# Attention joined over its batches, early first loads, and the turned maxima split by GpSimd

## The chip, the cores and the metric

The kernel runs on one core of a Trainium2 chip. The metric is the device time of one execution in microseconds. Three runs of the kernel before gave 2043.46, 2043.80 and 2047.93 us, a median of 2043.8 us.

## What is computed

The input `x` is 4 batches of 1024 tokens with 128 channels. Four residual layers follow one another: an attention with 16 heads of 8 channels, a mixture of experts, a gated delta layer with convolutions, and the same mixture of experts again. The change touches the first layer alone:

```python
x = x + attn_a(layernorm(x))
    q, k, v = x @ Wq.T, x @ Wk.T, x @ Wv.T          # 16 heads of 8
    q_c, k_c = q - mean(q), k - mean(k)             # over the 8 channels
    cov = einsum('bhqd,bhkd->bhqk', q_c, k_c) / 8
    var = outer(sum(q_c^2) / 7, sum(k_c^2) / 7) / 8
    attn = softmax(cov + var, axis=-1)
    out = (attn @ v) @ Wo.T
x = x + moe(layernorm(x)); x = x + attn_b(layernorm(x)); x = x + moe(layernorm(x))
```

A head's score is thus a product over 9 rows (8 channels and the variance). The rows are kept in three bf16 parts each, and 81 products of parts stand one below the other, so that one bf16 matmul gives the score with nearly the accuracy of f32.

## The kernel before, in words

**The projection, `project_qkv`.** 8 chunks of 512 tokens. Each chunk is normalised, turned and projected; ScalarE and VectorE split q, k and the variances into three bf16 parts, and SyncE's queue stores the parts in DRAM (`scr.terms`), four transfers for each chunk: two at L424, two at L428. The part tiles are double, so ScalarE waits before chunk c until the transfers of chunk c - 2 have landed (`s_out`). GpSimd meanwhile clears rows 64 to 127 of the operand tiles `q_op` and `k_op` (L311) and sets three rows of `k_op` to one (L315). The block ends when all transfers have landed.

**The attention, `attend`.** A unit is one batch with four heads (`GH`); there are 16 units, u = 4 b + s. The loads of a unit (L524 and L528) are 12 transfers, three of 216 KB and nine of 72 KB. In a unit:

- `scores_for_max` (L567): 32 tiles of 128 queries by 1024 keys, 8 matmuls each, into two buffers of `ps_max`; `reduce_max` (L696) takes the negated maximum of each query on VectorE. TensorE writes a tile when the reduction of the tile two before is done (`s_maxed`). This runs 40 tiles ahead (one unit and `LEAD` = 8).
- `turn_max` (L621) transposes the 32 columns of maxima. `split_max` (L707 to L714, VectorE) copies them out of PSUM and splits them into three bf16 parts by five operations that each need the one before. `max_rows` (L535) has SyncE's queue put the three parts as three rows into `q_op`, so that the second scores come out with the maximum subtracted.
- `scores_for_prob` (L582): 64 tiles of 128 keys by 512 queries, 4 matmuls each, into two buffers of `ps_prob`. The first of a unit waits for the three rows (`s_nmrow`). ScalarE takes the exponential (L684) into a ring of 16 tiles.
- `pv` (L599): the exponentials times v, four heads in four strips of `ps_acc`. A unit has two halves of 512 queries; each half sums over 8 key tiles.
- After a half, ScalarE copies `ps_acc` to SBUF in two pieces (`copy_acc`, L667), TensorE turns it by four matmuls with 36 columns of the identity (`combine`, L611) into `ps_misc`, and VectorE divides by the row sums (`normalise`, L719 and L725).

**The order.** TensorE's stream is written out by hand in 32 steps for each unit. Step i holds the two halves of one max tile, two probability tiles, one after the other in turn, and one piece of `pv` that lies `PV_LAG` = 3 steps back. As there is a single `ps_acc`, the first piece of a half (due in steps 3 and 19) is held back and made together with the second in steps 4 and 20, behind the wait for `copy_acc`. `combine` follows in the same steps, `turn_max` of the next unit in step 25. ScalarE puts the copies before exponentials 7 and 8 of a half, VectorE puts `normalise` in steps 6 and 22 and `split_max` in step 26.

**The loop over batches.** `batches` writes out batch 0 and batch 3 and puts batches 1 and 2 into a loop of the hardware (`Fori`), on every engine, with offsets and semaphore values in registers. So units 0 to 3 and 12 to 15 are straight code, and units 4 to 11 are two passes of one body.

## Time and profile before

| | |
|---|---|
| median of three runs | 2043.8 us |
| the profiled execution, its own time | 2043.38 us |
| its span on the core | 2041.7 us |
| projection, last transfers landed | about 92 us |
| attention, first loads to last operation | 92 to 912 us |
| TensorE matmul, busy over the span | 1361.8 us (67%) |
| VectorE | 1540.1 us (75%) |
| ScalarE | 917.1 us (45%) |
| GpSimd | 227.3 us (11%) |

The table of the page has the busy time of an engine over the whole span. It is an average over layers that are bound by different engines, so it only says where to look: in the 820 us of the attention, TensorE, VectorE and ScalarE all show nine tenths or seven to nine tenths of each slice. Which of them sets the pace has to be read from the idle time of the others and from what ended it. A row of the timeline has the start in us, the time in us to the end of the last of its instructions, the engine (PE is TensorE, PEld its weight load, DVE VectorE, ACT ScalarE, POOL GpSimd, SP SyncE; a q behind it marks its sequencer), the line, the tiles and shapes, the count, and in brackets the idle time before it with what released it.

### The profile page before, as it was taken

The page shows a single profiled execution, that of the slowest core. Times are in us where ns is not written, and L with a number is a line of the kernel's source. Part 1 is how long each engine was busy: PE and PEld are TensorE (multiplying, and loading weights), DVE is VectorE, ACT ScalarE, POOL GpSimd, SP SyncE. Part 2 cuts the span into 40 slices and gives each one's busy share as a digit, 9 for nine tenths or more (in the row PEclk, how much of TensorE's full clock was granted, in tenths as well). Part 3 has the DMA queues.
Part 4 walks back from the last instruction along what each step waited for, and adds up shares of the span by engine and source line. Part 5 has one row for each costly group of instructions (what it writes and reads, how often), then busy time and mean ns, then how long its engine had stood idle before and what let it go on. Part 6 is the DMA issues. An engine that isn't in the chain of part 4 may idle for free. (4 is left out here: it accounts for less than half of the span.)

```text
span 2041.7 us, 44670 instructions
## 1 busy us (share of the span) xinstructions
PE 1361.8 (67%) x15216; PEld 723.2 (35%) x15216; DVE 1540.1 (75%) x3117; ACT 917.1 (45%) x2009; POOL 227.3 (11%) x218
## 2 busy tenths in 40 slices
PE   4489999999999999984399674000000078841998
PEld 2214444444444444443166442000000024420665
DVE  5598888888788888707166576899999899972665
ACT  4507777777677777774143273001222200030343
POOL 6000000000000000003414300000000000025044
PEclk9858999999999999997699876555555589965999
DMA  3430111111111110003224415810222010012243
GB/s 98 120 80 5 40 41 30 29 29 29 30 29 29 29 29 3 3 20 96 60 55 66 75 67 117 212 41 10 63 63 54 19 41 0 0 43 58 55 67 44
DMA packets 118670, 101.05 MB, mean 49 GB/s; under 512 B 23665, under 2 KB 100018, under 8 KB 118066
## 3 DMA queue, kind: packets, MB, share of 16 engines
q1 hardware_dynamic: 101570, 84.79, 16.2%
q0 software_dynamic: 11264, 8.92, 3.0%
q10 hardware_dynamic: 5616, 4.47, 1.3%
q8 instruction: 130, 2.13, 0.4%
q14 instruction: 90, 0.74, 0.1%
HBM read 55.98 MB, written 31.21 MB: 43 GB/s over the span
## 5 line engine op out<-in xcount | busy, mean ns | idle before, releaser
L696 DVE TENSOR_REDUCE att_negmax<-att_ps_max 128x1 f32<-128x1024 f32 x512 | 613.9, 1221 | 112.5 <-PE att_ps_max L567 91.8
L684 ACT ACTIVATE att_probs<-att_ps_prob 128x512 f32<-128x512 f32 x1024 | 561.4, 598 | 244.7 <-PE att_ps_prob L582 233.8
L567 PE MATMUL att_ps_max<-av_k_op,av_q_op 81*32 81x512 bf16 x4096 | 418.0, 404 | 43.1 <-DMA av_q_op<-terms_q 18.9
L582 PE MATMUL att_ps_prob<-av_q_op,av_k_op 99*32 99x512 bf16 x4096 | 406.9, 385 | 9.2 <-ACT att_probs L684 1.2
L599 PE MATMUL att_ps_acc<-att_probs,att_vq 128*32 128x256 f32 x4096 | 308.3, 381 | 0.0
L1926 PE MATMUL out_ps_y<-all_bo_row,all_ones 1*128 1x128 f32 x2 | 0.8, 482 | 372.8 <-PEq L104 372.8
L567 PEld LDWEIGHTS att_ps_max<-av_k_op,av_q_op 81*32 81x32 bf16 x4096 | 109.4, 98 | 184.2 <-DVE att_negmax L696 80.6
L582 PEld LDWEIGHTS att_ps_prob<-av_q_op,av_k_op 99*32 99x32 bf16 x4096 | 108.1, 95 | 174.1 <-ACT att_probs L684 129.7
L599 PEld LDWEIGHTS att_ps_acc<-att_probs,att_vq 128*32 128x32 f32 x4096 | 126.4, 111 | 82.3 <-issue 5.8
L1145 ACT ACTIVATE moe_moe_gate<-moe_moe_ps_h 128x256 f32<-128x256 f32 x122 | 46.8, 383 | 214.2 <-PE moe_moe_ps_h L1086 214.2
L1926 PEld LDWEIGHTS out_ps_y<-all_bo_row,all_ones 1*128 1x128 f32 x2 | 0.5, 305 | 373.1 <-issue 373.1
L1086 PE MATMUL moe_moe_ps_h<-all_w_all,moe_moe_xgT 128*128 x244 | 128.0, 607 | 1.4 <-DVE moe_moe_xgT L1286 1.4
L1310 DVE TENSOR_TENSOR moe_moe_y<-moe_moe_y,moe_moe_ps_y 128x128 f32 x182 | 52.4, 288 | 89.3 <-issue 81.0
L1835 ACT ACTIVATE solve_p<-solve_state,solve_decay 128x32 f32<-128x32 f32 x128 | 45.0, 351 | 155.7 <-DVE solve_state L1819 155.7
L1101 PE MATMUL moe_moe_ps_y<-all_w_all,moe_moe_hT 128*128 x728 | 111.6, 276 | 0.3
L1101 PEld LDWEIGHTS moe_moe_ps_y<-all_w_all,moe_moe_hT 128*128 128x128 f32 x728 | 95.7, 192 | 1.5 <-issue 1.5
L1286 DVE COPY moe_moe_xgT<-moe_moe_ps_g 128x256 f32<-128x256 f32 x92 | 38.2, 415 | 69.4 <-PE moe_moe_ps_g L1079 69.4
L511 POOL COPY att_vq<-av_v 128x288 f32<-128x288 f32 (+1 forms) x16 | 6.8, 427 | 728.6 <-PE att_ps_acc L599 728.5
L1079 PE MATMUL moe_moe_ps_g<-all_ident,moe_moe_xin 128*128 128x128 f32 x182 | 36.5, 280 | 69.8 <-DMA moe_moe_xin<-expert_rows 69.6
L1944 PE MATMUL out_ps_o<-out_qS,out_gather 128*128 128x512 f32 x128 | 65.0, 632 | 25.8 <-DVE out_qS L2035 25.7
L1302 DVE SCALAR_TENSOR_TENSOR moe_moe_hs<-moe_moe_gate,moe_moe_scale,moe_moe_ps_h 128x256 f32<-128x256 f32 x122 | 58.3, 478 | 20.2 <-ACT moe_moe_gate L1145 20.0
L2029 DVE TENSOR_TENSOR_SCAN out_St<-b_a,out_kd 128x1024 f32<-128x1024 f32 x32 | 73.1, 2284 | 0.4
(277 smaller groups left out, 2067.4 us busy)
## 6 DMA issues: line engine op xcount, KB each, us to landing
moe_moe_xin<-expert_rows SPq DMA_DIRECT2D x182, 72.0 KB, 1.8
av_k_op<-terms_k SPq DMA_DIRECT2D x48, 216.0 KB
av_q_op<-terms_q SPq DMA_DIRECT2D x144, 72.0 KB
solve_dec_and_windows<-solve_Xw SPq DMA_DIRECT2D x16, 256.0 KB, 3.0
solve_dec_and_windows<-solve_k SPq DMA_DIRECT2D x16, 256.0 KB, 3.7
terms_q<-qkv_parts_q SPq DMA_DIRECT2D x8, 384.0 KB, 2.6
terms_k<-qkv_parts_k SPq DMA_DIRECT2D x8, 384.0 KB, 3.2
all_w_all<-in_f_w SPq DMA_DIRECT2D x24, 128.0 KB, 2.5
```

The source lines that it names most:

```text
L567: mm = pe.matmul(ps_max[c * STRIP:(c + 1) * STRIP, a % 2, k * CH:(k + 1) * CH], q_op[s][0:R_ALL, h, at:at + STRIP], k_op[s][0:R_ALL, h, k ...
L582: mm = pe.matmul(ps_prob[c * STRIP:(c + 1) * STRIP, j % 2, :], k_op[s][0:R_END, h, at:at + STRIP], q_op[s][0:R_END, h, half * CH:(half + 1 ...
L599: mm = pe.matmul(ps_acc[32 * h:32 * h + 32, cols], vq[:, s % 2, kt, VW * h:VW * h + 32], probs[:, (GH * v + h) % PROBS, cols], start=(kt = ...
L684: act.activation(probs[:, j % PROBS, :], ps_prob[:, j % 2, :], ACT.Exp).then_inc(s_exp, 1)
L696: dve.tensor_reduce(negmax[:, s % 2, a:a + 1], ps_max[:, a % 2, :], AX.X, ALU.max, negate=True).then_inc(s_maxed, 1)
L1086: pe.matmul(ps_up[n % 3][:, :, :].rearrange("p w f -> p (w f)"), xgT[:, n // 2 % 3, cols], wall[:, bass.ds(at0, 2 * F)], start=True, stop= ...
L1101: mm = pe.matmul(ps_y[n % 2][:, 0:P], hT[:, n % 3, i * P:(i + 1) * P], wall[:, bass.ds(at0 + (2 * F + i * P), P)], start=(i == 0), stop=(i ...
L1145: act.activation(gate[:, n % 3, :], ps_up[n % 3][:, 0, :], ACT.Silu).then_inc(s_silu, 1)
L1302: dve.scalar_tensor_tensor(out=hs[:, n % 3, :], in0=gate[:, n % 3, :], scalar=scale[:, n:n + 1], in1=ps_up[n % 3][:, 1, :], op0=ALU.mult, ...
L1310: dve.tensor_tensor(tile, tile, ps_y[n % 2][:, 0:P], ALU.add).then_inc(s_sum, 1)
L1944: mm = pe.matmul(ps_o[:, i * CH:(i + 1) * CH], gather[:, e, :, :].rearrange("p h d -> p (h d)"), qS[:, e % 2, i * CH:(i + 1) * CH], start= ...
L2029: dve.tensor_tensor_scan(St[:, e % 2, :], a[:, tok], kd[:, e % 2, :], 0.0, ALU.mult, ALU.add).then_inc(s_S, 1)
```

## The change

- `batches` is a Python loop over all four batches: no loop of the hardware is left in `attend`, on any engine. The store loop of `project_qkv` is written out too.
- The loads of units 0 and 1 are issued on SyncE's queue within `project_qkv`: eight transfers (two groups of `load_terms`) after each of the stores of chunks 2, 3 and 4. Before the first of them the queue waits for the stores of chunks 0 and 1 and for all of GpSimd's clearing. `attend` loads units 2 and 3 at its start.
- `ps_acc` becomes two banks, one for each half; `ps_misc` is gone. The first piece of `pv` is made in its own step. `combine` is four transposes of 128 columns that write into the bank of the half itself; `turn_max` writes into the bank of the first half.
- The pieces of `copy_acc` stand before exponentials 6 and 8.
- The turned maxima are copied by ScalarE (`take_max`), before exponential 54 of a unit (step 27), and the five operations of the split run on GpSimd (`split_max`), behind its copy of v.
- `normalise` is one reciprocal and one product where it was one reciprocal and four products.

The diff, cut to its core:

```diff
+            early = [(s, i) for s in range(EARLY) for i in range(NPART)]
+            for c in range(NC_):
+                store(c)
+                if c == 2:
+                    for p in range(2):
+                        sp.wait_ge(s_out[p], 16 * NDMA)
+                    sp.wait_ge(s_ones, 1 + 3 * NQ)
+                if c >= 2:
+                    for s, i in early[2 * (c - 2):2 * (c - 1)]:
+                        load_terms(sp, g, scr, 0, s, i)
...
+EARLY = 2
...
-COPY_AT = 2 * PV_LAG + 1
+COPY_AT = 2 * PV_LAG
...
-        ps_acc = m.ps("ps_acc", [P, CH])
-        ps_misc = m.ps("ps_misc", [P, CH])
-        comb = ps_misc[:, P:P + CT * GH * VW].rearrange("p (t g r) -> p t g r", t=CT, g=GH)
+        ps_acc = [m.ps(f"ps_acc{half}", [P, CH]) for half in range(2)]
+        comb = [a[:, :].rearrange("p (t g r) -> p t g r", t=CT, g=GH) for a in ps_acc]
...
-            body(0, True, False)
-            with eng.Fori(1, last_b) as b:
-                body(b, False, False)
-            body(last_b, False, True)
+            for b in range(B):
+                body(b, b == 0, b == last_b)
...
+            def split_max(u):
+
+                pool.wait_ge(s_split, u + 1)
+                if u >= 2:
+                    pool.wait_ge(s_nmrow, 16 * NPART * (u - 1))
+                chain = Count(pool, s_nmch, 4 * u)
+                rows, rest, parts = nm_rows[:, :], nm_rest[:, :], nm_parts[:, u % 2]
+                chain.done(pool.tensor_copy(parts[:, 0, :], rows))
+                chain.done(pool.tensor_tensor(rest, rows, parts[:, 0, :], ALU.subtract))
+                chain.done(pool.tensor_copy(parts[:, 1, :], rest))
+                chain.done(pool.tensor_tensor(rows, rest, parts[:, 1, :], ALU.subtract))
+                pool.tensor_copy(parts[:, 2, :], rows).then_inc(s_nmp, 1)
...
-                    if kt == 0 and not (isinstance(b, int) and b == 0 and s == 0 and half == 0):
-                        pe.wait_ge(s_acc, 2 * u + half)
+                    if kt == 0:
+                        if half == 0:
+                            pe.wait_ge(s_split, u + 1)
+                        elif u:
+                            pe.wait_ge(s_norm, 2 * u)
...
-                    mm = pe.matmul(comb[:, t], acc_sb[:, half, t * P:(t + 1) * P],
-                                   g.ident[:, :].rearrange("p (g r) -> p g r", g=GH)[:, :, 0:VW],
-                                   start=True, stop=True)
+                    mm = pe.transpose(ps_acc[half][:, t * P:(t + 1) * P], acc_sb[:, half, t * P:(t + 1) * P],
+                                      g.ident[:, :])
...
-                        for w in (w - 1, w) if w % (2 * TB) == 1 else () if w % (2 * TB) == 0 else (w,):
-                            if w >= 0:
-                                pv(b, s, w // 2, w % 2)
-                            elif not (first and s == 0):
-                                pv(*prev(b, s), (w + STEPS) // 2, w % 2)
+                        if w >= 0:
+                            pv(b, s, w // 2, w % 2)
+                        elif not (first and s == 0):
+                            pv(*prev(b, s), (w + STEPS) // 2, w % 2)
...
+            def take_max(u):
+                act.wait_ge(s_nmT, u + 1)
+                if u:
+                    act.wait_ge(s_nmp, u)
+                act.activation(nm_rows[:, :], ps_acc[0][0:STEPS, 0:P], ACT.Copy).then_inc(s_split, 1)
...
-                        if COPY_AT <= j <= COPY_AT + 1 and not (first and s == 0):
-                            copy_acc(*prev(b, s), 1, j - COPY_AT)
+                        if j == 2 * (STEPS - LEAD + 3) and not (last and s == NQ - 1):
+                            take_max(u + 1)
+
+                        if j in (COPY_AT, COPY_AT + 2) and not (first and s == 0):
+                            copy_acc(*prev(b, s), 1, (j - COPY_AT) // 2)
...
-                        if i == STEPS - LEAD + 2 and not (last and s == NQ - 1):
-                            split_max(*nxt(b, s, 1))
```

## Rows read from the trace of the kernel before

**Rows 1.** Waits from 150 to 1060 us: who waited for whom, total us, times, longest.

```profile
ACT att_probs L684 <- PE att_ps_prob L582: 233.8, 386, 60.9
```

**Rows 2.** Timeline of ScalarE in two steps of unit 2.

```profile
282.76 1.08 ACT L684 ACTIVATE att_probs<-att_ps_prob 128x512 f32<-128x512 f32 x2 [0.22 <-PE att_ps_prob L582]
...
284.07 1.09 ACT L684 ACTIVATE att_probs<-att_ps_prob 128x512 f32<-128x512 f32 x2 [0.22 <-PE att_ps_prob L582]
```

**Rows 3.** A stretch of unit 2: length, busy us of PE, PEld, DVE, ACT, POOL.

```profile
294.10:296.00 1.90, 1.90 (x40) 1.00 (x36) 1.89 (x2) 1.46 (x4) 0.00 (x0) 1.00 0.00 0
```

**Rows 4.** L684 alone, from unit start to unit start (units 2, 7, 8, 9).

```profile
250.25:297.16 46.91, 35.04 (x65) 1.00 0.14 32
...
486.34:538.16 51.82, 35.04 (x65) 0.99 0.16 39
538.16:588.75 50.59, 35.36 (x65) 0.95 0.08 19
588.75:636.01 47.26, 35.04 (x64) 1.00 0.12 31
```

**Rows 5.** Timeline of steps 3 and 4 of unit 2, the change of halves.

```profile
254.17 0.60 ACT L684 ACTIVATE att_probs<-att_ps_prob 128x512 f32<-128x512 f32 x1 [0.22 <-PE att_ps_prob L582]
...
255.40 0.41 ACT L667 ACTIVATE att_acc_sb<-att_ps_acc 128x256 f32<-128x256 f32 x1
...
255.66 1.12 ACT L684 ACTIVATE att_probs<-att_ps_prob 128x512 f32<-128x512 f32 x2
...
256.95 1.08 PE L611 MATMUL att_ps_misc<-all_ident,att_acc_sb 128*128 128x36 f32 x8
...
257.96 0.40 PE L567 MATMUL att_ps_max<-av_k_op,av_q_op 81*32 81x512 bf16 x4
...
258.63 1.08 ACT L684 ACTIVATE att_probs<-att_ps_prob 128x512 f32<-128x512 f32 x2 [1.84 <-PE att_ps_prob L582]
```

**Rows 6.** Timeline of four transposes in the projection and what follows.

```profile
75.95 0.66 PE L355 MATMUL qkv_ps_x<-all_ident,qkv_xn 128*128 128x128 f32 x4 [1.07 <-ACT qkv_xn L324]
76.54 0.63 PE L377 MATMUL qkv_ps_var<-qkv_square_q,all_varsel 128*48 128x512 f32 x1
```

**Rows 7.** Timeline around the split of the maxima in unit 2.

```profile
289.74 0.27 DVE L707 COPY att_nm_rows<-att_ps_misc 32x128 f32<-32x128 f32 x1
...
291.31 7.29 DVE L696 TENSOR_REDUCE att_negmax<-att_ps_max 128x1 f32<-128x1024 f32 x6
291.41 1.78 SPq L535 DMA_DIRECT2D av_q_op<-att_nm_parts  x3
...
293.24 1.09 ACT L684 ACTIVATE att_probs<-att_ps_prob 128x512 f32<-128x512 f32 x2 [1.16 <-PE att_ps_prob L582]
```

**Rows 8.** GpSimd's groups up to 400 us: busy us, mean ns, idle before.

```profile
L179 POOL TENSOR_SCALAR_AFFINE_SELECT all_varsel<-all_varsel 128x16 f32<-128x16 f32 x16 | 3.2, 198 | 2.2
L511 POOL COPY att_vq<-av_v 128x288 f32<-128x288 f32 x4 | 1.7, 426 | 159.4 <-PE att_ps_acc L599 159.3
```

**Rows 9.** Line L535, the three rows of maxima: durations in ns, and time to landing.

```profile
L535 SPq DMA_DIRECT2D av_q_op<-att_nm_parts x48: 502/584/1269, 145.1 to 864.7; - x48
...
DMA to landing us min/median/max: 1.8/1.8/3.0
```

**Rows 10.** Timeline at the end of the first pass of the loop.

```profile
536.98 0.62 PE L567 MATMUL att_ps_max<-av_k_op,av_q_op 81*32 81x512 bf16 x4 [3.64 <-issue]
```

**Rows 11.** Timeline of the start of the attention, and GpSimd's clearing before it.

```profile
37.15 14.20 POOL L315 MEMSET av_k_op<- 3x4096 bf16 x4
...
92.25 0.29 SPq L524 DMA_DIRECT2D av_k_op<-terms_k  x1
...
103.80 1.90 PE L567 MATMUL att_ps_max<-av_k_op,av_q_op 81*32 81x512 bf16 x16 [18.86 <-DMA av_q_op<-terms_q]
```

**Rows 12.** Stretches: us, engines' busy us, then PEclk, DMA share, GB/s.

```profile
73.00:78.00 5.00, 3.93 (x19) 1.97 (x17) 2.22 (x5) 4.27 (x10) 0.00 (x0) 1.00 0.58 177
...
100.00:104.00 4.00, 0.20 (x4) 0.14 (x8) 0.00 (x0) 0.00 (x0) 0.00 (x0) 0.50 0.61 162
```

More of the change, by code:

```diff
@@ L430, in _, with store @@
-            repeat(sp, NC_ // 2, body)
+            def store(c):
+                i, p = c // 2, c % 2
+                tok = slice(c * CH, (c + 1) * CH)
+                for w in range(2):
+                    sp.wait_ge(s_p3[w][p], i + 1)
+                    sp.dma_start(scr.terms[w][:, 0:D, :, tok].rearrange("i d h t -> (d h) i t"),
+                                 parts[w][:, p, :, :]).then_inc(s_out[p], 16)
+                sp.wait_ge(s_v3[p], i + 1)
+                for w in range(2):
+                    sp.dma_start(scr.terms[w][:, D, :, tok].rearrange("i h t -> h i t"),
+                                 vparts[32 * w:32 * w + H, p, :, :]).then_inc(s_out[p], 16)
@@ L435, with load_terms @@
+def load_terms(sp, g, scr, b, s, i):
+    heads, tok, row = slice(s * GH, (s + 1) * GH), slice(b * S, (b + 1) * S), i * NPART * K1
+    sp.dma_start(g.k_op[s][row:row + NPART * K1, :, :],
+                 scr.terms[1][:, :, heads, tok].rearrange("j d h t -> (j d) h t")).then_inc(g.s_load[s], 16)
+    for j in range(NPART):
+        sp.dma_start(g.q_op[s][row + j * K1:row + (j + 1) * K1, :, :],
+                     scr.terms[0][i, :, heads, tok]).then_inc(g.s_load[s], 16)
 LEAD = 8
 PV_LAG = 3
-COPY_AT = 2 * PV_LAG + 1
+COPY_AT = 2 * PV_LAG
@@ L536, in max_rows @@
                                  nm_parts[:, s % 2, i, :]).then_inc(s_nmrow, 16)
-            for s in range(NQ):
+            for s in range(EARLY, NQ):
                 load(0, s)
@@ L577, in scores_for_prob @@
                     pe.wait_ge(s_nmrow, 16 * NPART * (u + 1))
-                if not (isinstance(b, int) and b == 0 and s == 0 and j < 2):
+                if not (b == 0 and s == 0 and j < 2):
                     pe.wait_ge(s_exp, 2 * STEPS * u + j - 1)
@@ L618, in turn_max @@
                 pe.wait_ge(s_maxed, STEPS * (u + 1))
-                if not (isinstance(b, int) and b == 0 and s == 0):
-                    pe.wait_ge(s_misc, 3 * u - 1)
-                pe.transpose(ps_misc[0:STEPS, 0:P], negmax[:, s % 2, :], g.ident[:, :]).then_inc(s_nmT, 1)
+                if not (b == 0 and s == 0):
+                    pe.wait_ge(s_norm, 2 * u - 1)
+                pe.transpose(ps_acc[0][0:STEPS, 0:P], negmax[:, s % 2, :], g.ident[:, :]).then_inc(s_nmT, 1)
             for a in range(STEPS):
@@ L652, in body @@
                             turn_max(*nxt(b, s, 1))
-            batches(pe, body)
+            batches(body)
             for w in range(STEPS - PV_LAG, STEPS):
                 pv(last_b, NQ - 1, w // 2, w % 2)
-            combine(last_b, NQ - 1, 1, last=True)
+            combine(last_b, NQ - 1, 1)
         @block.scalar
@@ L693, in reduce_max @@
                 dve.wait_ge(s_scored, STEPS * u + a + 1)
-                if a == 0 and not (isinstance(b, int) and b == 0 and s < 2):
+                if a == 0 and not (b == 0 and s < 2):
                     dve.wait_ge(s_nmT, u - 1)
@@ L2097, in build @@
         g.s_experts = m.sem("experts_loaded")
+        g.s_load = m.sems("terms_loaded", NQ)
         g.s_scat = m.sem("rows_scattered")
```

101 lines of the change are left out of this document (32 added, 69 removed).

## The prediction

> **What bounds the kernel now.** The chain that ended last covers only the final layer, so it says nothing here; I read the attention in three steps. First the waits: ScalarE stood idle 233.8 us in all before its exponentials, each time for TensorE's scores [rows 1]. Then the inside of a step: exponentials start at 282.76 and 284.07, 1.31 us apart, with 0.22 us of idle time before each pair [rows 2], and over 1.90 us TensorE is busy 1.90, VectorE 1.89 and ScalarE 1.46 [rows 3]. TensorE sets the pace and VectorE is just behind it: with only two buffers of max tiles, any extra work of VectorE beyond about half a us comes back as a stall of TensorE. Third, the units: a unit of straight code takes 46.91 us, one of the loop 47.26, and the two on either side of the jump back take 51.82 and 50.59 [rows 4]. Were a unit only its 32 steps, it would take 32 x 1.305 = 41.8 us. So 5.1 us of each unit lie between steps, and the change goes at these.
>
> **Change of halves (twice in a unit).** The exponentials of steps 3 and 4 start 258.63 - 254.17 = 4.46 us before the next step where two steps are 2.61: 1.85 us extra [rows 5]. Of it 1.01 us (256.95 to 257.96) is the eight matmuls of `combine` [rows 5]; the other 0.84 is TensorE running into ScalarE, since step 3 has no `pv` and the double piece in step 4 waits for both copies out of the one `ps_acc`. After the change `pv` has another bank and waits for nothing that is late: the maxima were read in step 27 of the unit before, and for the second half `normalise` ran in step 6. The copies cost ScalarE 0.26 us each (255.40 to 255.66 [rows 5]) against 0.22 us of idle time in a step [rows 2], so about 0.04 us is left over, which the double buffer takes. `combine` becomes four transposes; the same four in the projection, at the same clock, took 76.54 - 75.95 = 0.59 us to the next matmul [rows 6]. The second copy is done before exponential 8, a whole step's TensorE work ahead of `combine`. So a change of halves costs 0.62 us in place of 1.85: 1.23 less. There are 31 within the units (unit 0 has one): 31 x 1.23 = 38.1 us. In the last three, where no max tiles are left and ScalarE sets the pace, the gain is a little larger; I add 0.7. Sum 38.8. Bounds: as little as nothing of the 0.84 may go if another wait takes its place (then only 0.42 is gained each, 13 us), and no more than the whole 1.85 less 0.59 (39 us).
>
> **The split of the maxima leaves VectorE.** Six operations hold VectorE from 289.74 to 291.31, 1.57 us, and the exponentials two steps later have 1.16 us of idle time before them in place of 0.22: 0.94 us lost [rows 7, 2]. This stall goes in units 0 to 13 (in unit 14 VectorE has no tiles at that point): 14 x 0.94 = 13.2 us. ScalarE takes one copy of 32 x 128. It reads half the columns of the copy that cost 0.26 us [rows 5], so it fits in 0.22 us of idle time: taken at nothing, at most 0.05 x 15. Its wait is for a transpose that TensorE issued at the end of step 25, two steps earlier; only exponentials are queued behind it.
>
> **The new chain.** GpSimd now stands between the copy and the three rows. What is late next is SyncE's queue and then the first probability tile of the next unit, and all of TensorE's stream queues behind that one wait. The time there is: the copy before exponential 54 ends near 289.75, so GpSimd starts at about 289.85. The next unit starts at 297.16 [rows 4], its first probability tile 0.44 us earlier, and without the 0.94 stall that is 295.8. The three transfers take 2 x 0.6 us of issuing and then 1.8 us to land, 3.0 us [rows 7, 9]. That leaves 295.8 - 3.0 - 0.1 - 289.85 = 2.85 us for five dependent operations. The trace has no such operation on GpSimd. Its copy of 128 x 288 takes 0.43 us, a select of 16 columns 0.20, and dependent selects have 2.2 / 16 = 0.14 us between them [rows 8]. Between these two rows a copy of 128 columns is about 0.30 us. An operation with two inputs is unknown: from 0.28 us (as the row of 0.30 with nothing added) to 0.85 (twice the largest row). In all, 3 x 0.30 + 2 x (0.28 to 0.85) + 4 x 0.14 = 2.0 to 3.2 us. I take 0.45 each, near the one-input rows, since 128 columns are few beside the fixed part: 2.4 us, so no stall and 0.4 us to spare. GpSimd has nothing else in that stretch; its copy of v for the next unit was done early in the unit. A rule speaks against this edit: the Trainium skill, GPSIMD Engine Reference, section Performance versus the Vector engine, finds an operation with two inputs 1.96 times as long on GpSimd as on VectorE. No row of this trace shows one. By it each of the two would be an estimated 0.55 us and the sum unchanged, with a reserve of some 0.2 us.
>
> **The loop goes.** The two units at the jump back took 51.82 + 50.59 - 2 x 47.26 = 7.9 us more than their like; at the jump TensorE stood 3.64 us for nothing that the profile shows [rows 4, 10], and the granted clock of the next unit was 0.95. Straight units do not have this. The eight loop units are 0.35 us longer than straight ones [rows 4]: 2.8 us. Together 10.7. Longer code could stall in its fetching, but the eight straight units of before, which differ from the new ones only in number, have no such gap, so I add nothing.
>
> **Normalise and turn_max.** One product in place of four shortens a burst on VectorE that was nearly hidden. Beyond halves and split, 46.91 - 41.8 - 3.70 - 0.94 = 0.5 us is left in a straight unit, some 0.3 of it the transpose, which stays; I take 0.1 a unit, 1.5 us. In 43.4 us a unit, VectorE has 32 reductions at 1.21 us (7.29 us for six [rows 7]) and about 1.2 us more, 40 in all, so it stays behind TensorE.
>
> **The early loads.** The attention starts at 92.25 and TensorE's first scores at 103.80, released by the loads [rows 11]. With units 0 and 1 loaded the first scores start at about 92.4: 11.4 us less. The clock there is 0.50 [rows 12], and I leave it so, since TensorE still stands idle from the end of the projection. The price is on the queue in the projection. A chunk lasts 8 us; its stores are 0.88 MB at up to 177 GB/s, 5 us; two groups of loads are 0.88 MB at 162 GB/s, 5.5 us [rows 12]. So three chunks bring 10.5 us of transfers in 8, and the queue falls behind by some 2.5 us each, 7.5 at the most, and makes it good in the chunks 5 to 7. ScalarE waits for stores two chunks old, which have about 8 us of reserve, so I take nothing. If the loads share the engines worse than this, chunk 7 waits up to 3 us. The wait for the clearing costs nothing: it ends at 37.15 + 14.20 = 51.35 [rows 11], when the queue has just issued chunk 2's stores. `attend` now issues two unit loads fewer, and its own two are needed tens of us later.
>
> **The sum.** 38.8 + 13.2 + 10.7 + 1.5 + 11.4 = 75.6 us. From the profiled execution's own 2043.4 this gives 1967.8; the median of the runs, 2043.8, is 0.4 us above it. I forecast 1968 us. A unit should then take 43.4 us.
>
> **The rivals.** (a) GpSimd's chain is longer than 2.85 us, and the wait for the maxima takes the place of VectorE's stall at each of 15 unit starts. For it: the two-input operations are unmeasured and the reserve is small. Against it: every GpSimd row of that size is below 0.45 us. At 3.2 us it costs 15 x 0.35 = 5 us, at 3.8 us 14 us: about 1977, up to 1982. (b) The gain at the halves is smaller, because exponentials delayed by the copies hold TensorE, or the loads slow the projection: 0.3 us for each of 31 halves is 9 us, 3 us more from the projection: 1974 to 1980. (c) Slower than before: the same chain of GpSimd, but so slow that its stall eats everything. It decides from a stall of 75.6 / 15 = 5.0 us in each unit, a chain of 7.9 us, 1.5 us for each operation; at 2 us each it would be some 2080 us. Against it stand all its rows of this size, at under a third of that. (d) The change does not do what it says: TensorE is held by something else that I read as free, say `pv` waiting for `normalise`, and only the loop, the split and the loads gain: 36.8 us and 13 of the halves, 1994 us.
>
> **How the numbers follow.** Forecast 0.52, (a) 0.20, (b) 0.18, (d) 0.05, (c) 0.03; 0.02 for no change. The range goes from 1959, if the clock at the start comes up early and the copies hide entirely, to 1985, which takes in (a) and (b) with their bounds. A measurement of this kernel can tell 0.2%, 4 us, from no change. Faster by more: 0.95; within: 0.02; slower: 0.03.
>
> **What would show it.** First scores at about 92.4 us. Units of 43.4 us, all alike from 1 to 13, with no gap of several us in unit 7. The step after each `combine` late by 0.6 us. No idle time of TensorE before the first probability tile of a unit; if there is any, released by the transfers of the three rows, (a) holds, and GpSimd's five operations, starting about 7 steps' time before, give its size. No stall two steps after the transposed maxima. Chunk starts in the projection 8.0 us apart; if chunk 7 starts late, the queue was too full. I would be wrong most of all if a unit came out above 44.5 us.

## The result, and the profile after

The kernel after the change takes 1970.7 us, the median of four runs (1965.9 to 1973.3), beside 2043.6 us for the kernel before (four runs, 2041.3 to 2047.9). The ratio of after to before is 0.9638, with a 95% interval of 0.9613 to 0.9662. The forecast was 1968 us, within a range of 1959 to 1985.

The page of the profiled execution of after (its own time is 1971.24 us): span, busy time of the engines, and the two largest groups.

```profile
span 1969.5 us, 42398 instructions
...
PE 1324.6 (67%) x15088; PEld 718.6 (36%) x15088; DVE 1517.7 (77%) x2925; ACT 918.3 (47%) x2025; POOL 253.8 (13%) x298
...
L727 DVE TENSOR_REDUCE att_negmax<-att_ps_max 128x1 f32<-128x1024 f32 x512 | 620.9, 1223 | 66.0 <-PE att_ps_max L590 37.3
L715 ACT ACTIVATE att_probs<-att_ps_prob 128x512 f32<-128x512 f32 x1024 | 556.3, 595 | 128.7 <-PE att_ps_prob L605 126.5
```

The exponential is at L715 now (L684 before), its scores at L605, the maximum's scores at L590, `pv` at L625, `combine` at L635 and the reduction at L727. ScalarE's idle time before its exponentials is 126.5 us for TensorE's scores over the whole kernel. VectorE lost work (1540.1 to 1517.7 us) and GpSimd gained some (227.3 to 253.8 us), but these totals don't say where the 72 us between the profiled executions went. They have to be looked for by stage:

| stage, profiled execution, us | before | after | difference |
|---|---|---|---|
| start to TensorE's first scores of the attention | 103.80 | 93.27 | -10.5 |
| first scores to the attention's last operation | 808.70 | 744.85 | -63.9 |
| the layers behind | 1129.2 | 1131.4 | +2.3 |

The sum is -72.1 us, which is 1971.24 - 2043.38. The units, for after, by the exponentials alone from unit start to unit start (units 2, 7 and 8: stretch, length, busy us of ScalarE with its instructions, PEclk, DMA share, GB/s), and then the stretch behind the attention (length, busy us of PE, PEld, DVE, ACT and POOL with their instructions, PEclk, DMA share, GB/s):

```profile
232.27:275.83 43.56, 34.73 (x64) 1.00 0.15 34
450.32:493.87 43.55, 34.73 (x64) 1.00 0.13 33
493.87:537.51 43.64, 34.73 (x64) 1.00 0.14 33
...
838.10:1969.50 1131.40, 541.12 (x2487) 336.04 (x2487) 831.84 (x2215) 296.34 (x822) 185.61 (x162) 0.73 0.26 60
```

Units 7 and 8 took 51.82 and 50.59 us before, and unit 2 took 46.91 [rows 4]. Now units 1 to 13 all lie between 43.55 and 43.70 us. Unit 0 takes 45.27, as TensorE's clock is low at its start, and unit 14 takes 41.95.

The same stretch behind the attention in the kernel before:

```profile
912.50:2041.70 1129.20, 539.31 (x2487) 335.25 (x2487) 831.67 (x2215) 296.50 (x822) 185.88 (x162) 0.73 0.26 60
```

The instructions are the same. TensorE's granted clock falls to half over parts of this stretch, for 614 us of it in after and 607 us in before. Over the twelve kernels of this document, which all have the same layers there, the stretch takes 1128.1 to 1134.0 us, so the 2.3 us are within that scatter.

**The change of halves.** The timeline of unit 2 of after, one line for each group of like instructions: start, time to the end of the last, engine, line, tiles, shapes and count.

```profile
235.86 0.39 ACT L688 ACTIVATE att_acc_sb<-att_ps_acc 128x256 f32<-128x256 f32 x1
236.20 1.08 ACT L715 ACTIVATE att_probs<-att_ps_prob 128x512 f32<-128x512 f32 x2
237.17 0.39 ACT L688 ACTIVATE att_acc_sb<-att_ps_acc 128x256 f32<-128x256 f32 x1
237.51 1.09 ACT L715 ACTIVATE att_probs<-att_ps_prob 128x512 f32<-128x512 f32 x2
...
237.71 0.63 PE L625 MATMUL att_ps_acc<-att_probs,att_vq 128*32 128x256 f32 x8
238.27 0.66 PE L635 MATMUL att_ps_acc<-all_ident,att_acc_sb 128*128 128x128 f32 x4
238.86 0.40 PE L590 MATMUL att_ps_max<-av_k_op,av_q_op 81*32 81x512 bf16 x4
239.53 0.60 ACT L715 ACTIVATE att_probs<-att_ps_prob 128x512 f32<-128x512 f32 x1 [0.93 <-PE att_ps_prob L605]
```

The exponentials of step 3 start at 236.20 and those of step 4 at 237.51, 1.31 us apart as in any step, although both copies lie there. Step 4 carries four transposes (238.27 to 238.86, 0.59 us), and the next exponentials come 2.02 us later: this step is 0.70 us longer than the others. The second copy ends at 237.56, 0.7 us before the first transpose starts, so the copies hold nothing up. Before, the same two steps lost 1.85 us together [rows 5]. No other step of a unit is late but step 25, by 0.32 us, where `turn_max` transposes the maxima; that was so before too. Step 28, which lost 0.94 us [rows 7], is now 1.31 us.

**The new chain.** From the copy of the maxima by ScalarE to the first probability tile of unit 3; only the rows of the chain are shown.

```profile
268.96 0.25 ACT L696 ACTIVATE att_nm_rows<-att_ps_acc 32x128 f32<-32x128 f32 x1
...
269.28 0.28 POOL L531 CAST att_nm_parts<-att_nm_rows 32x128 bf16<-32x128 f32 x1 [32.98 <-ACT att_nm_rows L696]
269.65 0.42 POOL L532 TENSOR_TENSOR att_nm_rest<-att_nm_rows,att_nm_parts 32x128 f32<-32x128 f32 x1
270.13 0.28 POOL L533 CAST att_nm_parts<-att_nm_rest 32x128 bf16<-32x128 f32 x1
270.49 0.42 POOL L534 TENSOR_TENSOR att_nm_rows<-att_nm_rest,att_nm_parts 32x128 f32<-32x128 f32 x1
270.97 0.28 POOL L535 CAST att_nm_parts<-att_nm_rows 32x128 bf16<-32x128 f32 x1
271.28 1.77 SPq L558 DMA_DIRECT2D av_q_op<-att_nm_parts  x3
...
275.39 0.39 PE L605 MATMUL att_ps_prob<-av_q_op,av_k_op 99*32 99x512 bf16 x4
```

GpSimd's five operations take 271.25 - 269.28 = 1.97 us, a cast 0.28, a difference 0.42, some 0.07 from one to the next. From the first issue of the three transfers to the tile that needs them there are 4.11 us. In the kernel below where TensorE stands for these transfers, its matmul starts 3.09 us after the first issue (278.47 - 275.38), so about 1.0 us is in reserve here. That reserve isn't there at every start. The weight load of the first probability tile of unit 7:

```profile
449.87 0.10 PEld L605 LDWEIGHTS att_ps_prob<-av_q_op,av_k_op 99*32 99x32 bf16 x4 [0.39 <-DMA av_q_op<-att_nm_parts]
```

By the semaphore events of the trace the last of the three rows landed 4.14 us after the first issue there, in place of 3.04 us: the reserve was just used up, and unit 6 is the longest at 43.70 us. Units 8 to 10 had landings at 3.79 to 3.89 us. In the last unit (15) the tile starts 3.09 us after the first issue, with nothing to spare, but unit 14 is no shorter (41.95 us) in the kernel below where the rows come in good time.

**The start.** The first scores of after, and two stretches of the projection while early loads run (columns as above).

```profile
93.27 1.90 PE L590 MATMUL att_ps_max<-av_k_op,av_q_op 81*32 81x512 bf16 x16 [7.23 <-PEq L104]
...
64.00:72.00 8.00, 6.45 (x22) 2.51 (x20) 5.22 (x12) 5.80 (x13) 0.00 (x0) 0.93 0.76 208
72.00:80.00 8.00, 5.38 (x20) 2.48 (x20) 5.22 (x12) 5.69 (x13) 0.00 (x0) 1.00 0.67 205
```

The scores wait for no load any more: before, they waited 18.86 us for one [rows 11]. The transfers move 205 to 208 GB/s in these stretches, and the early loads are done by 78 us.

### The profile page after: what moved, and what is told of

It reads as the page before. It is cut to its first block and busy times, and to the rows that moved or that the text cites. A ratio compares the mean times of both kernels' runs of the same rounds, so it can differ in the third digit from the quotient of the medians.

```text
span 1969.5 us, 42398 instructions
## 1 busy us (share of the span) xinstructions
PE 1324.6 (67%) x15088; PEld 718.6 (36%) x15088; DVE 1517.7 (77%) x2925; ACT 918.3 (47%) x2025; POOL 253.8 (13%) x298
## 5 line engine op out<-in xcount | busy, mean ns | idle before, releaser
L727 DVE TENSOR_REDUCE att_negmax<-att_ps_max 128x1 f32<-128x1024 f32 x512 | 620.9, 1223 | 66.0 <-PE att_ps_max L590 37.3
L715 ACT ACTIVATE att_probs<-att_ps_prob 128x512 f32<-128x512 f32 x1024 | 556.3, 595 | 128.7 <-PE att_ps_prob L605 126.5
L590 PE MATMUL att_ps_max<-av_k_op,av_q_op 81*32 81x512 bf16 x4096 | 417.9, 401 | 13.2 <-PEq L104 7.2
L605 PE MATMUL att_ps_prob<-av_q_op,av_k_op 99*32 99x512 bf16 x4096 | 407.2, 382 | 2.7
L625 PE MATMUL att_ps_acc<-att_probs,att_vq 128*32 128x256 f32 x4096 | 313.4, 379 | 0.0
L590 PEld LDWEIGHTS att_ps_max<-av_k_op,av_q_op 81*32 81x32 bf16 x4096 | 111.9, 97 | 146.5 <-DVE att_negmax L727 44.9
L605 PEld LDWEIGHTS att_ps_prob<-av_q_op,av_k_op 99*32 99x32 bf16 x4096 | 108.7, 95 | 146.1 <-ACT att_probs L715 94.3
L625 PEld LDWEIGHTS att_ps_acc<-att_probs,att_vq 128*32 128x32 f32 x4096 | 130.3, 111 | 78.4 <-issue 0.5
L531 POOL CAST att_nm_parts<-att_nm_rows 32x128 bf16<-32x128 f32 x16 | 4.5, 284 | 546.6 <-ACT att_nm_rows L696 546.6
```

The lines of the kernel that those rows point to most:

```text
L590: mm = pe.matmul(ps_max[c * STRIP:(c + 1) * STRIP, a % 2, k * CH:(k + 1) * CH], q_op[s][0:R_ALL, h, at:at + STRIP], k_op[s][0:R_ALL, h, k ...
L605: mm = pe.matmul(ps_prob[c * STRIP:(c + 1) * STRIP, j % 2, :], k_op[s][0:R_END, h, at:at + STRIP], q_op[s][0:R_END, h, half * CH:(half + 1 ...
L625: mm = pe.matmul(ps_acc[half][32 * h:32 * h + 32, cols], vq[:, s % 2, kt, VW * h:VW * h + 32], probs[:, (GH * v + h) % PROBS, cols], start ...
L715: act.activation(probs[:, j % PROBS, :], ps_prob[:, j % 2, :], ACT.Exp).then_inc(s_exp, 1)
L727: dve.tensor_reduce(negmax[:, s % 2, a:a + 1], ps_max[:, a % 2, :], AX.X, ALU.max, negate=True).then_inc(s_maxed, 1)
```

## The experiments

Each kernel is one of the two with a single edit. Times are medians; the ratio is to the kernel before, run on the same chip, with its 95% interval. "Attention" is the time from TensorE's first scores to the attention's last operation in the profiled execution.

### The loop alone

The kernel before, with its batches written out and nothing else changed:

```diff
-            body(0, True, False)
-            with eng.Fori(1, last_b) as b:
-                body(b, False, False)
-            body(last_b, False, True)
+            for b in range(B):
+                body(b, b == 0, b == last_b)
```

> The kernel before with one edit: the batches are written out, no loop of the hardware. My theory (the jump back costs 7.9 us, the loop's body 0.35 us a unit): all units from 1 to 13 take 46.9 us, none has a gap, time 2033 us, 10.7 less than before. Rival (the gap in unit 7 comes from what runs at that time, the transfers of the next unit, and not from the jump): the gap of 4 us stays at the start of unit 8, and about 2040 us. Rival (longer code must be fetched and stalls): gaps at other places, no gain or a loss.

Measured: 2032.5 us, ratio 0.9949 (0.9932 to 0.9965), 11.6 us under the before of the same runs. Units 7 and 8 by the exponentials:

```profile
484.51:531.44 46.93, 35.03 (x64) 1.00 0.14 31
531.44:578.38 46.94, 35.03 (x65) 1.00 0.14 31
```

They are now like all others (46.92 to 46.95), with no gap. The attention takes 796.58 us, 12.1 less, of which 0.9 lies in unit 0 and goes with the clock at its start. So the loop cost about 11.2 us, against 10.7 in the sum. The idle time of 3.64 us at the jump [rows 10] is gone with the jump. The Trainium skill, Runtime: NRT & Kernel Launch, section Instruction fetch mechanics, says that a taken branch to a page outside the fetched ones forces a fetch before execution goes on, while straight code crosses its blocks nearly for free. Both traces agree with that: 3.64 us at the jump, and no gap of TensorE in the straight code, whose units lie within 0.03 us. That the jump is what costs is shown by this experiment; that TensorE waits for a fetch there isn't, since the profile names no releaser. The 0.35 us of each other unit in the loop is gone too, without a cause that the rows name.

### The split back on VectorE

The kernel after, with the copy and the five operations in VectorE's step 26 again, in place of ScalarE's copy and GpSimd's chain:

```diff
-            take_max(0)
...
-                        if j == 2 * (STEPS - LEAD + 3) and not (last and s == NQ - 1):
-                            take_max(u + 1)
...
+                        if i == STEPS - LEAD + 2 and not (last and s == NQ - 1):
+                            split_max(NQ * b + s + 1)
```

> The changed kernel with the copy and the split of the maxima back on VectorE in step 26, as before; all else as changed. My theory (each split stalls TensorE by 0.94 us because only two max tiles are buffered): units 0 to 13 are 0.9 us longer, 44.5 instead of 43.6, and the step two behind the split is 2.2 us instead of 1.31; 1984 us, 13 more than the changed kernel. Rival (VectorE now has slack, since it no longer lags from the changes of halves, so the split hides): under 0.3 us a unit, under 1975 us.

Measured: 1982.4 us, ratio 0.9705 (0.9689 to 0.9721). The timeline of unit 2 around the split, and the unit's length:

```profile
271.47 0.27 DVE L717 COPY att_nm_rows<-att_ps_acc 32x128 f32<-32x128 f32 x1
...
272.02 0.28 DVE L720 TENSOR_TENSOR att_nm_rest<-att_nm_rows,att_nm_parts 32x128 f32<-32x128 f32 x1
...
273.04 4.68 DVE L708 TENSOR_REDUCE att_negmax<-att_ps_max 128x1 f32<-128x1024 f32 x4
274.30 0.40 PE L576 MATMUL att_ps_max<-av_k_op,av_q_op 81*32 81x512 bf16 x4 [0.76 <-DVE att_negmax L708]
274.97 1.09 ACT L696 ACTIVATE att_probs<-att_ps_prob 128x512 f32<-128x512 f32 x2 [1.16 <-PE att_ps_prob L591]
```

```profile
234.33:278.89 44.56, 34.73 (x64) 1.00 0.14 33
```

The whole chain of waits is visible: VectorE's next reduction starts only at 273.04, TensorE stands 0.76 us for its buffer, and ScalarE stands 1.16 us for TensorE, the same figure as in before [rows 7]. A unit from 1 to 13 is 44.55 us, 0.95 longer, and step 28 alone 0.94. The attention is 14.3 us longer, where 14 x 0.94 = 13.2 had been summed: 12.3 us in units 1 to 13, 1.4 in unit 0, where the clock stays at half 1.1 us longer than in after, and 0.6 ahead of unit 0. This last part is the split of the first maxima, which the sum had left out.

### The order at the change of halves

Three kernels, each after with a part of the old order. The first holds back the first piece of `pv`, waits for `copy_acc` again (`s_acc`), and puts the copies before exponentials 7 and 8:

```diff
-COPY_AT = 2 * PV_LAG
+COPY_AT = 2 * PV_LAG + 1
...
+                        if 2 * u + half:
+                            pe.wait_ge(s_acc, 2 * u + half)
...
+                        for w in (w - 1, w) if w % (2 * TB) == 1 else () if w % (2 * TB) == 0 else (w,):
```

> The changed kernel with the old order at the change of halves: the first piece of pv held back to the next step, behind a wait for the copies of the half before, and the copies before exponentials 7 and 8. Two banks and the four transposes stay. My theory (0.84 of the 1.85 us of a change of halves is this order, 0.42 the transposes): a change of halves costs 1.5 us instead of 0.70, a unit 45.2 us, 1996 us. Rival (the whole gain came from the transposes and the missing wait only matters because VectorE lags): under 0.3 us for each half, under 1980 us.

Measured: 1994.3 us, ratio 0.9754 (0.9737 to 0.9770). The timeline of the change of halves in unit 2, and the unit's length:

```profile
239.79 0.10 PEld L605 LDWEIGHTS att_ps_prob<-av_q_op,av_k_op 99*32 99x32 bf16 x4 [0.64 <-ACT att_probs L718]
...
240.16 1.07 PE L627 MATMUL att_ps_acc<-att_probs,att_vq 128*32 128x256 f32 x16
...
241.17 0.66 PE L637 MATMUL att_ps_acc<-all_ident,att_acc_sb 128*128 128x128 f32 x4
...
242.42 1.09 ACT L718 ACTIVATE att_probs<-att_ps_prob 128x512 f32<-128x512 f32 x2 [1.42 <-PE att_ps_prob L605]
```

```profile
234.45:279.46 45.01, 35.04 (x65) 1.00 0.14 32
```

Steps 3 and 4 take 1.50 and 2.54 us, so a change of halves loses 1.42 us in place of 0.70: the old order costs 0.72 us each. Units are 45.01 us, and the attention is 23.4 us longer. The row at 239.79 shows the loss at its source: TensorE has run ahead through a step without `pv`, and its weight load waits 0.64 us for ScalarE to free a buffer. After that its 16 `pv` matmuls come in one piece.

The second keeps the old order but leaves out the wait:

```diff
-                        if 2 * u + half:
-                            pe.wait_ge(s_acc, 2 * u + half)
```

> As held_back_and_wait, but without the wait for the copies of the half before (the other bank is free): the first piece of pv is only held back to the next step, and the copies stand before exponentials 7 and 8. My theory (of the 0.72 us a half that the old order cost, most is TensorE running ahead in the step without pv and then waiting for ScalarE, which has four exponentials and two copies in two steps): a change of halves still costs 1.2 to 1.3 us against 0.70, a unit 44.7 us. Rival (the wait for the copies in the one bank was the cost): 0.70 to 0.80 us, a unit 43.6 us.

Measured: 1988.6 us, ratio 0.9726 (0.9697 to 0.9756). Steps 3 and 4 take 1.50 and 2.37 us, 1.25 us over two plain steps; units take 44.71. So of the 0.72 us only 0.17 is the wait for the copies. The other 0.55 is the held-back piece together with the old places of the copies, which the next kernel prices.

The third leaves the new order of TensorE and moves only ScalarE's copies to where they were, one exponential apart:

```diff
-COPY_AT = 2 * PV_LAG
+COPY_AT = 2 * PV_LAG + 1
...
-                        if j in (COPY_AT, COPY_AT + 2) and not (first and s == 0):
-                            copy_acc(*prev(b, s), 1, (j - COPY_AT) // 2)
+                        if j in (COPY_AT, COPY_AT + 1) and not (first and s == 0):
+                            copy_acc(*prev(b, s), 1, j - COPY_AT)
```

> The changed kernel with only the places of the two copies as before, ahead of exponentials 7 and 8; pv keeps its own step. My theory (with a pv in each step ScalarE has 0.22 us to spare in each and either place is nearly free): a change of halves costs 0.70 to 0.85 us, a unit 43.6 to 43.9 us, up to 5 us in all. Rival (the places were what held the old order up): 1.0 us or more, a unit 44.2 us.

Measured: 1976.3 us, ratio 0.9668 (0.9651 to 0.9686). A change of halves loses 0.82 us in place of 0.70, units are 43.85 us and the attention is 4.1 us longer. This part of the change, two exponentials between the copies in place of one, is worth 0.12 us each. If the parts add up, that leaves 0.43 us for the held-back piece; no kernel held it back with the copies in their new places.

### The combine with 36 columns

After, with matmuls against 36 columns of the identity in place of four transposes, in the new order (four calls in the code, eight instructions in the trace):

```diff
-                    mm = pe.transpose(ps_acc[half][:, t * P:(t + 1) * P], acc_sb[:, half, t * P:(t + 1) * P],
-                                      g.ident[:, :])
+                    mm = pe.matmul(comb[half][:, t, :, 0:VW], acc_sb[:, half, t * P:(t + 1) * P],
+                                   g.ident[:, :].rearrange("p (g r) -> p g r", g=GH)[:, :, 0:VW],
+                                   start=True, stop=True)
```

> The changed kernel with combine as before, matmuls with 36 columns of the identity (the trace of before has eight of them for one combine) in place of four transposes of 128 columns. My theory (1.01 us for eight against 0.59 for four): each step of combine is 2.42 us instead of 2.01, a unit 44.4 us, 13 us more in the attention, 1984 us. Rival (TensorE's time goes by columns, and 36 are fewer than 128): a unit of 43.6 us or less.

Measured: 1983.7 us, ratio 0.9703 (0.9678 to 0.9727). The `combine` of unit 2, what follows it, and the unit's length:

```profile
239.81 1.08 PE L635 MATMUL att_ps_acc<-all_ident,att_acc_sb 128*128 128x36 f32 x8
...
240.82 0.40 PE L590 MATMUL att_ps_max<-av_k_op,av_q_op 81*32 81x512 bf16 x4
```

```profile
233.81:278.30 44.49, 34.73 (x64) 1.00 0.13 33
```

From the first of the eight to the next matmul there are 1.01 us, where the transposes take 0.59; the step is 0.42 us longer, and the attention 15.7 us. 31 steps give 13.0 us of that; the rest lies mainly in unit 0, where the clock stays at half 2.1 us longer than in after, and in unit 11 (45.11 us), which was not looked into. Order and transposes together are 0.72 + 0.42 = 1.14 us, and the traces of before and after differ by 1.85 - 0.70 = 1.15. The two parts account for the whole.

### No early loads

After, with all loads in `attend` as before:

```diff
-EARLY = 2
+EARLY = 0
```

> The changed kernel with no unit loaded within the projection; all four are loaded at the start of the attention. My theory: the first scores start about 11 us after the attention does instead of at once, the chunks of the projection keep their 8.0 us, and the time is 11 us longer, 1982 us. Rival (the early loads crowd the queue and slow the projection by about 1 us, and the later loads then come sooner): the projection ends 1 us sooner than in the changed kernel and the time is only 8 to 9 us longer.

Measured: 1983.9 us, ratio 0.9702 (0.9686 to 0.9719). TensorE's first scores:

```profile
104.66 1.90 PE L590 MATMUL att_ps_max<-av_k_op,av_q_op 81*32 81x512 bf16 x16 [18.95 <-DMA av_q_op<-terms_q]
```

They come 11.4 us later than in after, the figure of the sum. The projection isn't any faster without the loads beside it: the chunks start 8.0 to 8.1 us apart in both. The rest is nearly alike, the attention 745.99 us and the units 43.6, but unit 6 takes 44.21: TensorE waits for three rows that landed late at its end (the last section has more of this).

### GpSimd's chain made longer

After, with n = 2 and n = 6 more casts in GpSimd's chain, each needing the one before:

```diff
-                chain = Count(pool, s_nmch, 4 * u)
+                chain = Count(pool, s_nmch, (4 + n) * u)
...
+                for _ in range(n):
+                    chain.done(pool.tensor_copy(parts[:, 0, :], rows))
```

> The changed kernel with two more dependent casts in GpSimd's chain (the first one repeated): 0.7 us longer. My theory (the three rows land about 1.05 us before the next unit's first probability tile needs them): the rows come 0.7 us later and nothing else changes, units of 43.6 us. Rival (the chain is already at its limit): 0.3 to 0.7 us a unit, 5 to 10 us in all.

Measured with two: 1972.9 us, ratio 0.9650 (0.9626 to 0.9674). The chain takes 2.66 us. Two units of this kernel by the exponentials, and then the start of unit 5:

```profile
231.42:274.98 43.56, 34.73 (x64) 1.00 0.16 33
318.60:363.57 44.97, 34.73 (x65) 1.00 0.15 37
```

```profile
363.12 0.40 PE L607 MATMUL att_ps_prob<-av_q_op,av_k_op 99*32 99x512 bf16 x4 [1.22 <-DMA av_q_op<-att_nm_parts]
```

Unit 2 is as long as in after: 0.69 us more on the chain cost nothing there. But units 4, 5 and 6 are 44.97, 44.46 and 44.26 us, and at their ends TensorE waits for the three rows. Unit 14 is 42.71 us in place of 41.95, since the last unit start has no reserve; the others from 1 to 13 are 43.5 to 43.7. The attention is 3.3 us longer.

> The changed kernel with six more dependent casts in GpSimd's chain: 2.05 us longer. My theory: 1.05 us of it is hidden, the rest is a wait of TensorE before the first probability tile of a unit, 1.0 us at each of 15 units, 15 us in the attention, 1986 us. Rival (all of it shows, 31 us, or none since the loads run a whole unit ahead): 2001 or 1971 us.

Measured with six: 1993.4 us, ratio 0.9755 (0.9733 to 0.9777). The chain takes 4.05 us. Two units (2 and 4), the issue of the three rows and the first probability tile of unit 3, and its wait among the waits of the attention (us in total, times, longest):

```profile
234.22:278.92 44.70, 34.73 (x65) 1.00 0.14 33
324.82:371.94 47.12, 34.84 (x64) 0.96 0.12 26
```

```profile
275.38 1.78 SPq L560 DMA_DIRECT2D av_q_op<-att_nm_parts  x3
...
278.47 0.40 PE L607 MATMUL att_ps_prob<-av_q_op,av_k_op 99*32 99x512 bf16 x4 [0.87 <-DMA av_q_op<-att_nm_parts]
```

```profile
PE att_ps_prob L607 <- DMA av_q_op<-att_nm_parts: 17.0, 15, 2.1
```

Now the wait stands at all 15 unit starts. Most units are 1.06 us longer: 4.05 - 1.97 = 2.08 us were added and about 1.0 was swallowed by the reserve. The attention is 24.8 us longer, where 15 x 1.06 would be 15.9. Most of the rest, 6.2 us, is in units 3, 4 and 5 (45.91, 47.12 and 47.14 us): the rows land late there, and in units 4 and 5 the granted clock is 0.96 as well. So this stall costs more than the excess of the chain.

### One tile less of lead

After, with `LEAD` = 7, so that the maxima are turned one step later, and ScalarE's copy left at the same exponential:

```diff
-LEAD = 8
+LEAD = 7
...
-                        if j == 2 * (STEPS - LEAD + 3) and not (last and s == NQ - 1):
+                        if j == 2 * (STEPS - LEAD + 2) and not (last and s == NQ - 1):
```

> The changed kernel with LEAD = 7, and the copy of the maxima one step earlier after their transpose, before exponential 54 as it is now. One max tile fewer is reduced before the first unit (1.19 us, VectorE's pace) and one more lies in the last units (0.2 us); the maxima of a unit are turned one step later, 1.31 us. The copy follows two half steps behind the transpose instead of four, so it stays where it is. My theory (the rows land 1.03 us before they are needed and the copy does not move): 1 us less in the attention, no wait at the starts of units except where a transfer lands late; 1970 us. Rival (the copy now waits for the transpose and the exponentials behind it are late): 0.2 us a unit more, 2 to 4 us longer than the changed kernel.

Measured: 1968.3 us (five runs, 1964.8 to 1972.9), ratio 0.9634 (0.9618 to 0.9650). The attention is 744.26 us, 0.6 less than in after, and the units are 43.61. The traces say that it is no worse; the times can't tell it from after.

## Why the prediction was right, point by point

**Change of halves: 31 x 1.23 forecast, 31 x 1.15 found.** The mechanism was right in both its parts. Order: 0.84 was named, 0.04 of it given back for the copies, and 0.72 was lost when the old order came back. The prediction put this down to two causes at once, a step without `pv` and the wait for the copies. The runs part them: 0.55 (0.12 of it the places of the copies) and 0.17. Transposes: 0.42 forecast, 0.42 measured, because the duration had come from the same four transposes in the projection [rows 6]. The term that was mis-sized is what stays: 0.62 us was forecast for a change of halves, and it is 0.70, 31 x 0.08 = 2.5 us over the attention. It isn't the copies, for which 0.04 had been put down: they hide. It is the way into `combine`. The forecast counted from the first transpose to the next matmul, 0.59 us. But the first transpose starts 0.31 us after the start of the last `pv` matmul, where the next scores start 0.19 us after it in a plain step. These 0.12 us stand ahead of the eight matmuls of before as well (again 0.31), so they were counted in the 0.84 and can't be gained: 0.84 - 0.12 is the 0.72 that the order gave.

**The split: 13.2 us forecast, 14.3 us lost when it was put back.** The stall of 0.94 us [rows 7] returned as 0.94. The rest is the first split, 0.57 us ahead of unit 0, and the clock in unit 0.

**The loop: 10.7 us forecast, 11.6 us between the medians, about 11.2 in the trace.**

**The new chain: no stall forecast, none of more than 0.1 us a unit found.** The estimate was 2.4 us in a bound of 2.0 to 3.2, and it takes 1.97. The unmeasured operation was the difference with two inputs, taken at 0.45 us: it is 0.42. The reserve was forecast at 0.4 us; it is 1.0 when the rows land in 3.04 us, since the chain was 0.4 us shorter than taken. The transfers were taken at 3.0 us always, and this is the weak step: at four unit starts of after they took 3.8 to 4.1 us. With the reserve of 0.4 us that was forecast, these would have been stalls. That the chain came out short enough to cover them was luck. The time there was for it, 2.85 us by the sum, comes out as 1.97 + 1.0 = 3.0. The rule cited with the prediction (the Trainium skill, GPSIMD Engine Reference, section Performance versus the Vector engine, an operation with two inputs 1.96 times as long as on VectorE) has that figure from 2048 elements, and it doesn't hold for the 128 columns here: VectorE takes 0.28 us for it in the kernel with the split put back, and GpSimd 0.42, 1.5 times.

**Normalise: 0.1 us a unit.** It wasn't tried alone. The remainder of 0.5 us in a unit of before is 43.6 - 41.8 - 2 x 0.70 = 0.4 us now, 0.32 of it in step 25, which agrees with 0.1. Steps 8 and 24, two behind each `normalise`, point the same way: 1.37 us each in unit 2 of before and with the loop alone gone, 1.31 in after and also in the kernels with the old order or the split put back. That is 0.12 us a unit.

**The early loads: 11.4 us forecast; 10.5 in the trace of after, 11.4 against the same kernel without them.** The first scores were due at 92.4 and came at 93.27. About 1.0 us went in the projection between the first and the second chunk: by ScalarE's squares of q their starts are 9.56 us apart, and 8.56 in before. That is at 27 to 37 us, before any early load is issued (the first is at 52.9), and the granted clock rises at 31.0 us there, in place of 28.1. The eight other kernels with the same early loads follow that time: where the clock rose at 28.4 to 29.0 us (five of them) the scores started at 92.39 to 92.63, where it rose at 29.8 at 92.83, and at 31.1 and 31.2 at 93.25 and 93.45. So this is a scatter of the clock's start and no price of the loads. The loads themselves cost the projection nothing. That the queue would fall behind by up to 7.5 us and catch up in time was too dark, and it came from a wrong reading. The sum took 177 GB/s as the rate of the stores [rows 12], but this is the mean of 5 us in which the stores start late and run out. Two single microseconds of the same stretch of before (columns as above):

```profile
74.00:75.00 1.00, 0.88 (x8) 0.69 (x7) 0.61 (x1) 1.00 (x3) 0.00 (x0) 1.00 1.03 339
75.00:76.00 1.00, 0.05 (x1) 0.05 (x1) 0.08 (x1) 1.00 (x4) 0.00 (x0) 1.00 0.91 313
```

Stores alone reach 339 GB/s. A chunk's stores and two groups of loads are 1.76 MB by the sum, and at the 205 to 208 GB/s that the stretches of after show they take some 8.5 us, an estimate. So the queue falls behind by some 0.5 us a chunk and not by 2.5.

**The sum.** Inside the attention 75.6 - 11.4 = 64.2 us was forecast, and 63.85 came. That this is so close is partly luck. The changes of halves gave some 2.5 us less than forecast. Unit 0 made up for it with 3.58 us where 1.23 + 0.94 + 0.1 = 2.3 was due: the clock is at half for its first 7.1 us, and for 10.1 us before. The first split gave 0.57 us ahead of it, and the loop 0.5 more than its term. The 2.7 us between the forecast and the median are less than the spread of after's own runs, 7.3 us. The profiled execution is 3.4 us above its sum of 1967.8: the late start (0.9 us), the attention (0.3) and the 2.3 us of the layers behind, which execute the same instructions. Why those layers take 1128.1 us in one kernel and 1134.0 in another isn't settled. The time at half clock alone doesn't order them: with the shorter lead it is 620 us and the layers take 1129.7, in after 614 us and 1131.4.

**The rivals.** (a), a chain longer than the time there is, doesn't hold for this change, but its mechanism is real. With 2.66 us it appears at five unit starts (three units are longer by 0.6 to 1.4 us, a fourth by 0.1, and unit 14 by 0.8), with 4.05 us at all 15. Its price was underrated: the prediction took the excess times 15, which gives 15.9 for six casts where 24.8 us were lost. (c) needed a chain of 7.9 us; (d) would have left a wait at a change of halves, and there is none. (b), a smaller gain at the halves, holds in sign with a quarter of its size (0.08 us each, not 0.3), but not by its mechanism, since the copies delay nothing in their new places; its other half, loads slowing the projection, falls.

## What to carry to other kernels

Cut the cost of a unit into the excess of each step over the plain pace, and name for each the engine that is late; the three that were taken away here (1.15 of 1.85, 0.94 and the jump) gave back what the trace had said, to within 1 to 3 us each. Operations that keep the pacing engine waiting can go to an idle engine even if that takes longer for each of them, as long as the whole chain, its transfers with it, ends before the next need; count that reserve, and leave it larger than the scatter of a transfer's landing, which was 1.1 us at one start here. A piece of work held back to be done in double later can cost more than the wait that it was made for: here some 0.43 against 0.17 us. Before a mean rate is taken for a queue's speed, cut its stretch into single microseconds.

## What the runs showed of the hardware that was not expected

**The landing of three small transfers scatters, and it goes with instruction fetches.** Each of the three rows moves 8 KB from SBUF to SBUF, and normally the last packet is there 2.61 us after the first issue and the semaphore tells of it at 3.04. With two more casts in the chain there were four unit starts where the last packet came 3.1 to 3.65 us after it. The transfers of that kernel by queue, in the stretch of one of them (358 to 363 us; packets, MB, share):

```profile
q8 instruction: 1, 0.02, 1.4%
```

In each of the four, a packet of 16 KB of instructions had been fetched 0.7 to 2.4 us after the first issue. At the neighbouring unit starts, where it fell 0.3 us before the issue or 4.6 us behind it, the rows were on time. The same holds for the traces of after and of the nine kernels made from it, 150 unit starts without the first. In 40 of them a packet of 16 KB of instructions starts within 2.6 us behind the first issue, and in all 40 the rows land late, 3.2 to 4.8 us after the issue by the semaphore. Of the other 110 starts, five are late, by 0.6 us at most. The late starts move from kernel to kernel with the fetches: unit starts 7 to 10 in after, 4 to 6 and 11 and 12 with 36 columns, 8 to 10 and 15 with the split put back. That is strong, but no run moved a fetch alone, and what in the fetch delays the rows isn't shown.

**A stall can be followed by a lower clock.** A stall of 0.9 us at each unit start mostly leaves the clock at full, while units 4 and 5 of the kernel with six more casts show 0.96 and take 2.4 us more than the others. Here the stall comes first. TensorE had waited 2.1 us for the rows until 324.37; then came (PE, PEld, DVE, ACT and POOL, PEclk, DMA share, GB/s):

```profile
324.30:325.30 1.00, 0.93 (x20) 0.51 (x24) 0.26 (x1) 0.47 (x1) 0.00 (x0) 1.00 0.65 178
325.40:328.70 3.30, 3.30 (x40) 1.36 (x32) 2.09 (x2) 1.70 (x4) 0.00 (x0) 0.50 0.59 133
```

TensorE was back at work for 1.0 us before the clock fell to half for 3.4 us. The next start is alike: a wait of 1.7 us until 371.49, half clock from 373.15. But the start of unit 6, with the same wait of 1.7 us, is followed by no fall, so the length of the stall alone doesn't decide. Of the 2.4 us some 0.8 are the longer stall at the unit's end, and the rest goes with the clock.
